# Linear attention of a fused decoder kernel: the next group's projections issued ahead of the numerators

## The reference

```python
def _L1_xattn_ref(query, key, value, attention_mask, Wq, bq, Wk, bk, Wv, bv, Wqf, Wkf, Wo, bo):
    q, k, v = heads(query, Wq, bq), heads(key, Wk, bk), heads(value, Wv, bv)   # 16 heads of 16
    q_prime = relu(einsum('bhnd,fd->bhnf', q, Wqf))                            # 64 features
    k_prime = relu(einsum('bhnd,fd->bhnf', k, Wkf)) * attention_mask
    kv = einsum('bhnf,bhne->bhfe', k_prime, v)
    qkv = einsum('bhmf,bhfe->bhme', q_prime, kv)
    qk_sum = einsum('bhmf,bhf->bhm', q_prime, sum(k_prime, axis=2))
    return merge_heads(qkv / (qk_sum + 1e-8)) @ Wo.T + bo

x = x + _L1_xattn_ref(_layernorm(x), ctx, ctx, mask, ...)     # this stage
x = x + _L1_ffn_ref(_layernorm(x), ...)                        # the expert mix behind it
```

## Time and profile before

| what | value |
|---|---|
| median of three runs | 958.34 us (958.18 to 958.46) |
| the profiled execution, its own time | 958.29 us |
| its span in the trace | 956.5 us |
| TensorE matmul busy over the span | 934.4 us (98%) |
| VectorE busy | 621.8 us (65%) |
| ScalarE busy | 480.4 us (50%) |

### The profile page before, as it was taken

The page is one execution under the profiler, slowest core; times in us unless marked ns, Lnnn a source line. Parts: engine busy times, 40 slices in busy tenths (PEclk is TensorE's granted clock), DMA queues, the critical chain, the costliest instruction groups (busy, mean ns, idle before and its releaser), DMA issues.

```text
span 956.5 us, 20070 instructions
## 1 busy us (share of the span) xinstructions
PE 934.4 (98%) x7659; PEld 793.8 (83%) x7659; DVE 621.8 (65%) x1376; ACT 480.4 (50%) x1610; POOL 239.2 (25%) x261
## 2 busy tenths in 40 slices
PE   9999999999999999999999999999999999999988
PEld 7677778899788888888888888888888897777767
DVE  5878887897865566564456464556446655777864
ACT  4887877444445554444444443434444554444642
POOL 2556796671011111111111011101111122110000
PEclk9999999999999999999999999999999999999999
DMA  8100000002430000000000000010002002100002
GB/s 305 49 2 2 2 2 2 2 1 91 137 128 1 2 1 1 1 1 1 1 1 2 1 1 1 1 62 1 1 1 89 1 1 112 68 2 2 3 1 88
DMA packets 11325, 28.02 MB, mean 29 GB/s; under 512 B 1856, under 2 KB 7264, under 8 KB 10720
## 3 DMA queue, kind: packets, MB, share of 16 engines
q1 hardware_dynamic: 10512, 26.48, 7.8%
q10 hardware_dynamic: 720, 0.27, 0.1%
HBM read 24.65 MB, written 2.10 MB: 28 GB/s over the span
## 4 chain that ended last, share of the span: by engine, by line
PE 87%; DVE 8%; ACT 3%; issue 2%; POOL 0%; POOLq 0%; DVEq 0%
PE bank L50 16%; PE bank L52 14%; PE bank L51 14%; PE bank L2242 6%; PE bank L2191 5%; PE bank L405 3%; PE bank L415 3%; PE bank L2232 3%; PE bank L2115 2%; PE bank L2106 2%; PE bank L427 2%; PE bank L180 2%; PE bank L1651 2%; PE bank L1084 1%; PE bank L1102 1%
## 5 line engine op out<-in xcount | busy, mean ns | idle before, releaser
L2047 POOL TENSOR_TENSOR wa_prob<-wa_prob,wa_rsum 128x512 f32<-128x512 f32 x64 | 67.5, 1055 | 405.3 <-DVE wa_rsum L2630 405.3
L2424 ACT ACTIVATE wa_prob<-wa_prob,wa_negmax 128x128 f32<-128x128 f32 x256 | 99.8, 391 | 66.5 <-DVE wa_negmax L2619 66.2
L50 PE MATMUL bank<-norm_xT_hi,wide_hi 128*128 128x512 f32 x256 | 105.9, 414 | 0.2 <-DVE norm_xT_lo L191 0.2
L51 PE MATMUL bank<-norm_xT_lo,wide_hi 128*128 128x512 f32 x256 | 101.0, 395 | 0.0
L52 PE MATMUL bank<-norm_xT_hi,wide_lo 128*128 128x512 f32 x256 | 101.0, 395 | 0.0
L2686 DVE TENSOR_TENSOR wa_z_lo<-bank,wa_z_hi 128x512 fp32r<-128x512 f32 x64 | 44.3, 692 | 86.8 <-ACT wa_z_hi L2458 86.4
L606 ACT ACTIVATE v_prob<-bank,la_negmax 128x128 f32<-128x128 f32 x256 | 91.1, 398 | 1.5 <-DVE la_negmax L693 1.5
L2432 ACT COPY wa_q<-bank 128x512 f32<-128x512 f32 x64 | 37.6, 587 | 93.6 <-PE bank L52 93.6
L2439 ACT COPY wa_v<-bank 128x512 f32<-128x512 f32 x64 | 37.3, 584 | 89.5 <-PE bank L52 89.4
L337 POOL TENSOR_TENSOR v_prob<-v_prob,la_rsum 128x512 f32<-128x512 f32 x64 | 66.5, 1040 | 49.1 <-DVE la_rsum L698 48.9
L2242 PEld LDWEIGHTS bank<-wa_probT,wa_v 128*128 128x128 f32 x512 | 65.4, 191 | 10.7 <-DVE wa_probT L2673 5.0
(11 more groups left out here) (287 smaller groups left out, 2378.3 us busy)
## 6 DMA issues: line engine op xcount, KB each, us to landing
wide_raw<-in_wide_w SPq DMA_DIRECT2D x16, 512.0 KB, 6.8
em_w<-in_em_w SPq DMA_DIRECT2D x1, 4096.0 KB, 13.3
lc_kt<-in_ctx_rev SPq DMA_DIRECT2D x1, 2048.0 KB, 10.3
lc_toep<-in_toeplitz SPq DMA_DIRECT2D x1, 2048.0 KB, 14.4
li_kt<-in_ctx_rev SPq DMA_DIRECT2D x4, 512.0 KB, 6.5
out_x<-x SPq DMA_DIRECT2D x8, 256.0 KB, 2.5
x<-in_x SPq DMA_DIRECT2D x3, 512.0 KB, 5.1
h_or_w<-in_li_w SPq DMA_DIRECT2D x1, 1024.0 KB, 5.0
```

What stands on the lines that cost most here:

```text
L50: nc.tensor.matmul(out, a[0], b[0], start=start, stop=False, skip_group_check=True)
L51: nc.tensor.matmul(out, a[0], b[1], start=False, stop=False, skip_group_check=True)
L2047: nc.gpsimd.tensor_tensor(prob[:, s], prob[:, s], rsum[:, s, :].unsqueeze(2).to_broadcast([P, G, P]), ALU.mult).then_inc(prob_ok, 1)
L2424: last = nc.scalar.activation(prob[:, s, j, :], prob[:, s, j, :], ACT.Exp, bias=negmax[:, s, j:j + 1], scale=SCALE, accum_out=sums[:, s, j ...
```

## The change

One call moves in TensorE's program: `early(n)` stands directly behind `project(n - 1)`, ahead of `query_features` and of `numerators_and_denominators(n)`. With that, `numerators_and_denominators(n)` is followed at once by `key_values(n + 1)` (at the steps where the values are not done between them). The other engines' programs are as they were, and no instruction is added or removed. `early(13)` is called from the written-out tail, which isn't touched.

```diff
             ahead(n)
             if n > 0:
                 project(n - 1)
+            early(n)
             if t < NG and j >= 2:
                 query_features(t, j - 2)
             numerators_and_denominators(n)
-            early(n)
             if not VALUES_AHEAD[n]:
                 values(n + 2)
             key_values(n + 1)
```

## The result

The changed kernel takes 962.29 us (median of six runs, 961.94 to 962.52) against 958.35 us of the kernel before on the same chip (six runs, 958.18 to 959.09): a ratio of 1.004, 95% interval 1.0029 to 1.0051. It is slower by 3.9 us, where 4.0 was predicted (962.3).

A forecast was written before the change was run, and what follows sets the result against it. TensorE, busy 98% of the span, was taken as the bound. Step terms of 0, 0.98, 0.68, 0.49, 0.46 and 1.41 sum to 4.02 us, taking the 956.5 span to 960.5 and, with 1.79 around it, 962.3; range 960.3 to 963.9.

The forecast's parts named there:

- steps 1, 4, 5, 8, 9: saving against wait: Steps with j = 0 or 1: 0.19 saved in transitions, 0.20 waited for ScalarE's copy behind the denominators; nothing comes out.
- step 2: keys' copy behind the Relus: Step 2: `late` waits for ScalarE's copy, behind denominators and two Relus; 1.17 less 0.19, +0.98 us.
- step 6: Relus, quotient, key features' copy: Step 6: key features wait for Relus, projection for the quotient, next query features for VectorE's copy; +0.68 us.
- step 10: Relus: Step 10: key features wait for the Relus to free their banks; 0.68 less 0.19, +0.49 us.
- step 11: turn ahead of the numerators: Step 11: the mix's turn, 0.55, goes ahead of the numerators, less 0.09 of a saved entry; +0.46 us.
- step 12: turn waits for the norm: Step 12: the moved turn waits for VectorE's norm and holds back the numerators and second turn; +1.41 us.
- The transitions: TensorE going between blocks of different tile shapes: each moved block of products saves 0.19 us, 1.5 at eight steps.
- the first rival: Hand-overs dearer: no copy overlap with the denominators, projection-to-product transition costing 0.10; up to 1.6 us more, 963.9; chance 0.12.
- The waits: TensorE behind the numerators waiting for ScalarE or VectorE: 0.20 at five steps, longer at steps 2, 6, 10 and 12.
- The second rival: Transitions win at the ten steps: 1.7 us gain, 956.6; mild form 960.7, sharing 0.17 with the third rival; faster 0.04.
- T: The moment the numerators' last matmul ends on TensorE: their start plus 1.08 us, 858.43 at step 6 before the change.
- The third rival: Tail behind step 12 absorbs: VectorE up to 0.57 later, not 1.41; 961.5 us; chance 0.17 with the second's mild form.

The follow-up runs named there:

- the kernel that takes the waits away: Against the kernel before: products of steps 1, 2, 4, 5, 8 and 9 moved, ScalarE copying them ahead of denominators and Relus; 957.68 us against 958.66, ratio 0.9989.

## Why the prediction was right

The forecast named the mechanism term by term, and the terms came out, not only their sum. What the trace of the changed kernel gave, as shifts of TensorE against the kernel before:

| term | predicted | measured |
|---|---|---|
| steps 1, 4, 5, 8, 9: saving against wait | 0 | -0.07 |
| step 2: keys' copy behind the Relus | +0.98 | +0.86 |
| step 6: Relus, quotient, key features' copy | +0.68 | +0.73 |
| step 10: Relus | +0.49 | +0.49 |
| step 11: turn ahead of the numerators | +0.46 | +0.43 |
| step 12: turn waits for the norm | +1.41 | +1.41 |
| sum | 4.02 | 3.86 in the stretch, 3.9 in the medians |

The lines of the last column sum to 3.85; the hundredth to 3.86 is rounding. The five steps of the first line gave -0.03 when they alone were moved. Two small errors of opposite sign, at steps 2 and 6, help the sum a little.

**The transitions.** The saving of 0.19 a block is confirmed by the kernel that takes the waits away (4.43 against 4.61, and 1.21 us in the sum of six, once the norm is out of the way as well). L1102 directly in front of L1084 costs nothing, as the earlier trace rows had it. One detail was wrong in form: L50 starts 0.68 behind the projection and not 0.87, but its own first product then takes 0.42 to the next start instead of 0.24; from the projection to the numerators it is 2.36 (848.26 to 850.62), the figure the sum implies. So the end that would have cost 0.10 at each block did not come, and the first rival fell with it and with ScalarE's overlap: the copy starts 0.38 behind the denominators' start (851.76, 852.14), against 0.37 assumed.

The rule on drains that the prediction quotes (the Trainium skill, TensorEngine Tiling (Array Packing), Key Properties) fits the entries to and from the full array here, about 0.1 each; for a change from 32-column to 64-column tiles the trace shows no added time. It pointed the right way for the transitions and would have missed the result, since they are worth 1.7 and the waits 5.4.

**The waits.** Each was named with its place and releaser. The long ones are in the list of waits (1.09 at step 2, 0.60 and 0.61 behind steps 6 and 10, 1.14 at step 12); the five of 0.2 show only as 1.24 in place of 1.05 in front of `late`. The 0.05 for a signal stood on no row of the kernel before; the changed kernel shows it (the copy ends at 852.14 + 0.68 = 852.82, `late` starts at 852.87). The step 2 term was sized 0.12 too large: its wait came out as 2.22 - 1.05 = 1.17 between L1084 and L50, as summed, but before the change the query features of step 2 had waited for VectorE (1.04 behind the projection instead of 0.96), and the moved block covers that 0.08. The prediction saw such a wait only for step 7; the other 0.04 is not explained. The step 6 term was 0.05 too small, and its parts were weighed a little wrong: up to the projection it cost 0.52 and not 0.56, nearly all of it the Relus' and not the quotient's, and behind it 0.21 and not 0.12, since the query features start 1.29 behind the projection, not 1.2.

**The second rival** (transitions win) is not wrong as a mechanism but in where it decides: with ScalarE's copy first, six blocks bring 0.8 us, and 1.2 once VectorE's norm is moved too. At steps 6, 10, 11 and 12 the place of ScalarE's copy is not what decides: what is missing there is time behind the numerators. The key features wait for the Relus until T + 1.66 (steps 6, 10 and 11), the quotient of step 6 is there at T + 2.78, the norm that step 12 needs at T + 5.60, and the moved block was what TensorE did meanwhile. One reordering is left untested. The two Relus that end at T + 1.52 at step 6 read query features that were finished before T, and are late only because they stand behind the denominators' copy. Ahead of it they would free the banks sooner, but hold the denominators, and with them the quotient, back by up to their 1.08; no kernel here shows which weighs more. **The third rival** (the tail absorbs) fell in every profile: what lies behind the numerators of step 13 takes 47.3 us in all of them, and step 12 alone costs 1.42 of stretch and 1.5 us of time.

## What to carry to other kernels

Where an engine is busy all the time, ask of a block that is moved ahead what it was covering behind: here the numerators start a chain on two other engines, and what is taken from behind them opens a wait as soon as the chain is longer than the work that is left there. A product that is issued earlier gains nothing while its copy still stands, in the queue of the engine that takes it out, behind an instruction that waits for later work; move both, and then look which third engine becomes late. Going between full-array products and 32-column or 64-column tiles costs about 0.1 us here, so grouping tile shapes is worth doing only where it opens no wait.

## What the runs showed of the hardware

From full-array matmuls into 128x32 tiles costs 0.09 us (0.21 to the next start in place of 0.12), back from them 0.10 (0.33 in place of 0.24), from 128x32 to 128x64 tiles nothing (1.01 and 1.01 after). Two ScalarE activations back to back overlap by a tenth also when the first had to wait for its input (0.47 long, next start 0.38 later). And a full-array product of fp32r operands behind a float32 projection starts 0.68 us behind it, where 0.87 had been worked out, and takes 0.42 to the next start in place of 0.24, so that the 0.2 are given back at once: single start times of pipelined matmuls shift, sums over a block hold.
